# Transformer block on one core: V computed once per token and spread by SBUF to SBUF transfers, probabilities packed at 48 keys a block

## The reference, cut to what matters

```python
q, k, v = split_heads(xn @ qkv_w + qkv_b)            # 16 heads, head_dim 16
k_pad = jnp.pad(k, ((0, 0), (7, 7), (0, 0)))
v_pad = jnp.pad(v, ((0, 0), (7, 7), (0, 0)))
idx = jnp.arange(L)[:, None] + jnp.arange(15)[None, :]
scores = einsum('bld,blwd->blw', q, k_pad[:, idx]) / 4
out = einsum('blw,blwd->bld', softmax(scores, -1), v_pad[:, idx])
return merge_heads(out) @ proj_w + proj_b
```

## Time and profile before

| | |
|---|---|
| median of three runs | 2178.18 us |
| the profiled execution | 2176.03 us |
| its span, first to last instruction | 2174.3 us |
| around the span | 1.7 us |
| PE busy, PE weight loads busy | 95%, 87% |
| DVE, ACT, POOL busy | 73%, 50%, 48% |
| granted TensorE clock, mean | 0.99 |
| distance from one step to the next in the steady part | 131.3 us |

### The profile page before, as it was taken

How to read it: one execution, slowest core, us unless ns; L and a number is a source line. 1 busy time by engine, 2 the same in 40 slices (tenths; PEclk the granted TensorE clock), 3 DMA queues, 4 the chain that set the end, 5 groups by cost and what they waited for, 6 DMA issues and landing times.

```text
span 2174.3 us, 39417 instructions
## 1 busy us (share of the span) xinstructions
PE 2068.2 (95%) x13985; PEld 1883.4 (87%) x13985; DVE 1585.7 (73%) x3535; ACT 1095.1 (50%) x1716; POOL 1054.2 (48%) x993
## 2 busy tenths in 40 slices
PE   5689999999999999999999999999999999999999
PEld 4578898888988888898888989888898898988888
DVE  7568686786868768686785868868687786867843
ACT  3245554545555545554545545545455555545444
POOL 7544355544454534455444555534455443555435
PEclk9699999999999999999999999999999999999999
DMA  2111111111101111011111111111011111111111
GB/s 87 39 35 40 44 36 35 50 40 44 39 26 49 50 44 35 30 47 43 49 40 40 40 30 49 40 54 30 25 54 45 45 40 45 35 35 50 40 49 49
DMA packets 128881, 92.14 MB, mean 42 GB/s; under 512 B 9673, under 2 KB 127662, under 8 KB 128686
## 3 DMA queue, kind: packets, MB, share of 16 engines
q1 hardware_dynamic: 128686, 89.62, 13.9%
HBM read 81.20 MB, written 8.39 MB: 41 GB/s over the span
## 4 chain that ended last, share of the span: by engine, by line
PE 66%; DVE 24%; issue 6%; POOL 3%; ACT 1%; DMA 0%; DVEq 0%; ACTq 0%; POOLq 0%
PE psB L234 33%; PE psA L234 24%; DVE tm L606 10%; PE psA L1021 4%; DVE hr_lo L511 4%; PE psA L942 3%; DVE tm L622 1%; PE psA L1048 1%; DVE acc L525 1%; DVE smax L582 1%; DVE vb L562 1%; DVE smax L589 1%; DVE y L614 1%; DVE z_lo L539 1%; DVE st L501 1%
## 5 line engine op out<-in xcount | busy, mean ns | idle before, releaser
L511 DVE TENSOR_TENSOR hr_lo<-hf,hr_hi 128x512 fp32r<-128x512 f32 x512 | 469.3, 917 | 433.3 <-ACT hr_hi L828 431.2
L828 ACT ACTIVATE hr_hi<-hf 128x512 fp32r<-128x512 f32 x512 | 323.4, 632 | 316.4 <-PE psB L234 223.3
L403 POOL TENSOR_SCALAR wx_hi<-raw 128x512 fp32r<-128x512 f32 x256 | 168.5, 658 | 481.3 <-PE psB L234 470.4
L405 POOL TENSOR_TENSOR wx_lo<-raw,wx_hi 128x512 fp32r<-128x512 f32 x256 | 384.3, 1501 | 21.4
L824 ACT ACTIVATE hf<-psB,b1x 128x512 f32<-128x512 f32 x256 | 175.7, 686 | 278.5 <-PE psB L234 264.4
L418 POOL TENSOR_SCALAR kb<-kT,gmask 128x384 f32<-128x384 f32 x128 | 159.0, 1257 | 287.9 <-ACT kT L844 287.9
L234 PE MATMUL psB<-wx_hi,hr_hi 128*128 128x256 f32 x1024 | 288.8, 282 | 0.2
L234 PE MATMUL psB<-wx_hi,hr_lo 128*128 128x256 f32 x1024 | 287.1, 280 | 0.0
L234 PE MATMUL psB<-wx_lo,hr_hi 128*128 128x256 f32 x1024 | 287.0, 280 | 0.0
L606 DVE TENSOR_TENSOR tm<-psA,rinv 32x64 f32<-32x64 f32 x1024 | 225.8, 220 | 25.2 <-PE psA L1048 11.4
L234 PE MATMUL psB<-z_hi,wx_hi 128*128 128x512 f32 x512 | 212.3, 415 | 0.0
(11 more groups left out here) (158 smaller groups left out, 5470.7 us busy)
## 6 DMA issues: line engine op xcount, KB each, us to landing
raw<-in_L_ffn_W1e SPq DMA_DIRECT2D x256, 128.0 KB, 2.2
raw<-in_L_ffn_W2e SPq DMA_DIRECT2D x256, 128.0 KB, 2.1
xin<-in_L_attn_x SPq DMA_DIRECT2D x16, 512.0 KB, 3.7
out_x<-acc SPq DMA_DIRECT2D x32, 256.0 KB, 2.7
raw<-in_L_attn_fc_w SPq DMA_DIRECT2D x8, 256.0 KB, 2.8
raw<-in_L_ffn_W1m SPq DMA_DIRECT2D x4, 256.0 KB, 2.7
raw<-in_L_ffn_W2m SPq DMA_DIRECT2D x4, 256.0 KB, 2.8
raw<-in_L_attn_qkv_w SPq DMA_DIRECT2D x4, 192.0 KB, 4.5
```

What stands on the lines that cost most here:

```text
L403: g.tensor_scalar(wx[0][:, s, :], raw[:, s, :], 1.0, 0.0, ALU.mult, ALU.add).then_inc(w_hi.sem, 1)
L405: g.tensor_tensor(wx[1][:, s, :], raw[:, s, :], wx[0][:, s, :].bitcast(f32), ALU.subtract).then_inc(w_lo.sem, 1)
L511: v.tensor_tensor(hr[1][:, c % 2, :], hf[:, c % 3, :], hr[0][:, c % 2, :].bitcast(f32), ALU.subtract).then_inc(h_lo.sem, 1)
L828: a.activation(hr[0][:, c % 2, :], hf[:, c % 3, :], ACT.Copy).then_inc(h_hi.sem, 1)
```

## The change

V is computed once per token: two calls of `values`, n = 0 and 1 at q 3 and 4, each for two adjacent tiles of 128 tokens. DVE adds the bias in one instruction of 128x512 a call and writes `vs`, tokens on partitions. Then SP issues six transfers from `vs` to `vb` (`windows`), at its q 3, behind the loads of that q; all six increment one semaphore, and PE's `attend(t, 0)` waits for all of them. They have 7, 41, 48, 48, 39 and 9 partitions, with 12 or 16 runs of 64 floats (256 B) on each. A block has 48 places in `pr`, so two blocks are 96 columns: `turn` makes 96 rows, ACT copies 96, and `attend` works on 96 partitions of `pT` and `vb`. The blocks of a unit stand in their natural order (`place` is gone). The mask `keep` and the zero fill of `pr` are gone.

```diff
-        vb = sb("vb", [P, NB // 2, KD * G, P])
-        pr = sb("pr", [P, 2, 2, G, 4, 64])
+        vs = sb("vs", [P, NT, D])
+        vb = sb("vb", [PK, 2, NT, KD * G, P])
+        pr = sb("pr", [P, 2, 2, G, 4, KW])
...
+            def windows(t):
+
+
+                sp.wait_ge(vs_s.sem, vs_s.all(t))
+                if t:
+                    sp.wait_ge(av.sem, av.all(t - 1))
+                for half, j, key, at, n, tiles, back in (
+                        (0, 0, 0, P - RAD, RAD, range(1, NT), 1), (0, 0, RAD, 0, KW - RAD, range(NT), 0),
+                        (0, 1, 0, QB - RAD, KW, range(NT), 0), (1, 0, 0, 2 * QB - RAD, KW, range(NT), 0),
+                        (1, 1, 0, 3 * QB - RAD, QB + RAD, range(NT), 0), (1, 1, QB + RAD, 0, KW - QB - RAD, range(0, NT - 1), -1)):
+                    sp.dma_start(vb[KW * j + key:KW * j + key + n, half, tiles[0]:tiles[-1] + 1, :, 64 * j:64 * j + 64].rearrange("p i g n -> p (i g) n"),
+                                 vs[at:at + n, tiles[0] - back:tiles[-1] + 1 - back, :].rearrange("p i (g n) -> p (i g) n", n=64)
+                                 ).then_inc(vb_in.sem, 16)
...
+                    if q == 3 and t < ROWS:
+                        if t == 0:
+                            sp.wait_ge(zeroed.sem, 1)
+                        windows(t)
...
-            g.memset(pr[:, :, :, :, :, :], 0.0).then_inc(zeroed.sem, 1)
-            g.memset(vb[:, :, :, :], 0.0).then_inc(zeroed.sem, 1)
+            g.memset(vb[:, :, :, :, :], 0.0).then_inc(zeroed.sem, 1)
...
             def values(t, n):
                 v.wait_ge(val.sem, val.at(t, n))
                 if t:
...
+                    v.wait_ge(vb_in.sem, vb_in.all(t - 1))
+                v.tensor_tensor(vs[:, 2 * n:2 * n + 2, :], psA[:, 2, :].rearrange("p (i n) -> p i n", n=D),
+                                bv[:, :].unsqueeze(1).to_broadcast([P, 2, D]), ALU.add).then_inc(vs_s.sem, 1)
...
-                    base = LEFT - RAD + (4 * n + j) * QB
+                    to = LEFT + (2 * n + j) * P
...
                 for g in range(G):
                     pe.wait_ge(pT_s.sem, pT_s.at(t, 2 * u + g))
                     if g == 0:
-                        pe.wait_ge(vb_s.sem, vb_s.at(t, (11, 15, 15, 15)[u]))
+                        pe.wait_ge(vb_in.sem, vb_in.all(t))
...
                     elif q == 7:
                         turn(t, 0)
-                        pe.wait_ge(vb_s.sem, vb_s.at(t, 7))
-                        values(t, 2)
...
                     elif q == 10:
                         scores(t, 3)
-                        pe.wait_ge(att.sem, att.at(t, 0))
-                        values(t, 3)
```

More of the change, by code:

```diff
@@ L36, in build @@
     KW = 48
+    PK = 2 * KW
     G = 2
@@ L110, in build @@
         ones = one[:, :].to_broadcast([1, P])
-        keep = sb("keep", [P, 3])
         bv = sb("bv", [P, D])
@@ L241, in chunk_weights @@
             return ([[w[:, s, k * P:(k + 1) * P] for w in wx] for k in range(KD)], [w[:, s, KD * P:] for w in wx])
-        def place(j):
-            return 2 * (j % 2) + j // 2
         def unit_scores(u):
-            return pr[:, u % 2, :, :, :, 0:KW].rearrange("p t g b k -> p (t g b) k")
+            return pr[:, u % 2, :, :, :, :].rearrange("p t g b k -> p (t g b) k")
         HALVES = (range(0, NT // 2), range(NT // 2, NT))
@@ L600, in attend @@
                         src = psA[QB * h:QB * h + QB, 2:4, :].rearrange(
-                            "p g (t j s n) -> p g t j s n", t=2, j=2, s=2)[:, :, :, b % 2, b // 2, HD * h:HD * h + HD]
+                            "p g (t j s n) -> p g t j s n", t=2, j=2, s=2)[:, :, :, b // 2, b % 2, HD * h:HD * h + HD]
                         dst = tm[QB * b:QB * b + QB, 2 * th:2 * th + 2, c * P:(c + 1) * P].rearrange(
                             "p t (g n) -> p g t n", g=G)[:, :, :, HD * h:HD * h + HD]
-                        w = rinv[QB * h:QB * h + QB, u, :, :, :].rearrange("p t g b -> p g t b")[:, :, :, place(b)]\
+                        w = rinv[QB * h:QB * h + QB, u, :, :, :].rearrange("p t g b -> p g t b")[:, :, :, b]\
                             .unsqueeze(3).to_broadcast([QB, G, 2, HD])
@@ L869, in turned @@
                         a.wait_ge(av.sem, av.at(t - 1, 6 + g))
-                    a.activation(pT[:, g, :, :].rearrange("p j q -> p (j q)"), psA[:, g, :], ACT.Copy).then_inc(pT_s.sem, 1)
+                    a.activation(pT[0:PK, g, :, :].rearrange("p j q -> p (j q)"), psA[0:PK, g, :], ACT.Copy).then_inc(pT_s.sem, 1)
             for t in range(ROWS + 1):
@@ L996, in values @@
                 for j in range(2):
-                    base = LEFT - RAD + (4 * n + j) * QB
+                    to = LEFT + (2 * n + j) * P
                     for k in range(KD):
-                        last = three(pe, psA[:, 2, j * D:(j + 1) * D], [z[:, k, base:base + P] for z in zT], [w[:, k, 2 * D:] for w in wqkv],
+                        last = three(pe, psA[:, 2, j * D:(j + 1) * D], [z[:, k, to:to + P] for z in zT], [w[:, k, 2 * D:] for w in wqkv],
                                      k == 0, k == KD - 1)
@@ L1019, in scores @@
                         b = 4 * h + j
-                        dst = psA[:, h, 0:4 * G * KW].rearrange("p (g b k) -> p g b k", g=G, k=KW)[:, :, place(j), :]
+                        dst = psA[:, h, 0:4 * G * KW].rearrange("p (g b k) -> p g b k", g=G, k=KW)[:, :, j, :]
                         last = pe.matmul(dst, qm[:, th, b, :], kb[:, th, b, :].rearrange("p (g k) -> p g k", g=G), start=True, stop=True)
@@ L1032, in turn @@
                     for j in range(NP_):
-                        last = pe.transpose(psA[:, g, j * P:(j + 1) * P], pr[:, th, j // 2, g, 2 * (j % 2):2 * (j % 2) + 2, :].rearrange("p b k -> p (b k)"), ident[:, :])
+                        last = pe.transpose(psA[0:PK, g, j * P:(j + 1) * P], pr[:, th, j // 2, g, 2 * (j % 2):2 * (j % 2) + 2, :].rearrange("p b k -> p (b k)"), ident[:, :])
                     last.then_inc(trp.sem, 1)
@@ L1047, in attend @@
                     for j in range(NP_):
-                        last = pe.matmul(psA[:, 2 + g, j * P:(j + 1) * P], pT[:, g, j, :], vb[:, th * NP_ + j, c * G + g, :], start=True, stop=True)
+                        last = pe.matmul(psA[:, 2 + g, j * P:(j + 1) * P], pT[0:PK, g, j, :], vb[:, j % 2, 2 * th + j // 2, c * G + g, :], start=True, stop=True)
                     last.then_inc(av.sem, 1)
```

16 lines of the change are left out of this document (4 added, 12 removed).

## The result

The changed kernel takes 2325.1 us (median of four runs, 2323.2 to 2326.2) against 2178.1 us, 1.0675 times the time of before, 95% interval 1.0657 to 1.0694: slower by 147 us. The forecast was 2325.

What follows compares the result with a forecast made beforehand. PE's own work was taken to set a steady row, so new waits are paid in full. The profiled 2176.0 us plus 43.9 for row 0 plus 105 for 15 steady rows gave 2325 us; range 2275 to 2445.

Steps and rivals of the forecast that it cites:

- One engine for 41 partitions: The six transfers: engines get equal numbers of partitions, so 41, a prime, goes to one engine with 656 packets.
- Rival A: The six transfers: all engines share them evenly, 188 packets each; 2162 us, faster by 0.6%; chance 0.10.
- rule of 260 packets on the fullest engine: Transfers in steady rows: below about 260 packets on the fullest engine no steady row stalls.
- The start: SP's q 3: transfers stand behind load 7, issued every 0.57 us; PE comes to `attend(0)` at 435.26, 1.51 us earlier.
- The price of a packet: The transfers: 19 ns per 256 B packet, 812 packets on the fullest engine 15.4 us, plus 1.75 us fixed.
- Rival B: The transfers: a 256 B packet costs as much as one of 512 B, 28 ns; 2442 us; chance 0.17.
- The idles behind the stall: PE in the weighted sums of a steady row: DVE's head start removes two idles, minus 2.2 us.
- The clock: PE behind the stall: granted clock 0.50 for 3.5 us of work, adding 1.65 us to a steady row.
- A steady row: Counted on PE: 9.0 later, minus `values(3)` 1.5, minus idles 2.2, plus clock 1.65; +7.0 us, +105 in 15 rows.
- The other count, on DVE: Steady row: DVE starts 8.5 us later, minus 2.0 for the placements; sum 6.5 us.
- Row 0: Transfers wait in SP's queue behind the last dense piece and land at 88.9; transposes start at 117.1, 43.9 us later.
- No effect: Transposes and sum over keys, denser `mask`, `shift` and `exp`, and expert loads behind the transfers: 0.

Runs made afterwards that it cites:

- 40 + 1: Changed kernel with the transfer of 41 partitions cut into 40 and 1: 2179.7 us, 1.0009 of before.
- the doubled transfer: Changed kernel with the first transfer of 48 partitions cut into 47, also a prime, and 1: 2487.9 us.
- the kernel with the cut widths: Changed kernel with the transfers of 41 and 39 partitions cut into 32 + 9 and 32 + 7: 2187.4 us, 1.0049 of before.
- the last experiment: Kernel with split, early transfers and row 0 mended, plus DVE's gathers of units 2 and 3 ahead of that q's rounding difference: 2112.6 us, 0.9702 of before.
- the filler: Changed kernel with 28 useless matmuls of 512 columns on PE ahead of the first weighted sum of rows 1 to 15: 2284.2 us.
- early transfers: Changed kernel with the six transfers issued ahead of load 7 in steps from 1 on: 2169.9 us, 0.996 of before.
- either repair: Changed kernel with either the 41 and 39 partitions cut in two (2187.4 us) or the transfers issued ahead of load 7 (2169.9 us).
- both together with row 0's: Changed kernel with split transfers, issued ahead of load 7, and row 0's behind the first eight dense pieces: 2124.9 us, 0.9756 of before.

## Why the prediction was right, and where its terms were not

**The bound.** Right: PE's own work sets a steady row, so removed matmuls pay in full and a new wait costs in full. Without transfers, and with row 0's 40 us in it, the kernel takes 2169.3 us; 2178.1 + 40.1 - 45 is 2173. The 4 us between them stay open.

**One engine for 41 partitions.** Right, and the step that decided. It was an inference from a count of completion packets; the flat 18 GB/s, the 62 completion packets a row, the cuts into 32 + 9 and 40 + 1 and the doubled transfer bear it out. Rival A, even sharing, is the kernel with the cut widths, whose transfers are nearly even: 2187 us, not the 2162 I gave it. The sign of that rival was wrong too: with the late place it is no faster than before. Its own rule of 260 packets on the fullest engine failed too: the cut transfers have 216 there, and every row still stalls, because eight issues of 0.89 us make the last one late.

**The start.** Right: the transfers follow load 7, and PE arrived within 0.3 us of the time I gave, counted from `turn(0)` (8.42 us in row 3 for 8.17).

**The price of a packet.** Mis-sized. I took 19 ns, a duration from a straight line between 11 and 28 ns; the duration is 18, the long transfer's packets follow each other every 14.5 ns, and where all engines work it is 21. Against it, an issue of such a transfer takes about 0.9 us instead of 0.57, and SP stood, which I hadn't seen coming. Together the landing came 15.4 us after the first issue where I had 17.7, and the stall is 7.66 us on average, 8.80 in row 3, where load 7 itself went out slowly, for 10.5 forecast. This term was 2.8 us too large. Rival B, 28 ns, is out.

**The idles behind the stall.** Wrong, the step as I put it: "minus the two idles 2.2, which DVE's head start removes". They are there to a hundredth, 1.12 and 1.02 us for 1.15 and 1.03. A head start at the first unit doesn't reach them: each idle arises between two neighbours, PE's sum and DVE's gather, and the last experiment removes most of one by changing DVE's order. 2.2 us too little.

**The clock.** The mechanism was right, the size wrong: 1.65 us forecast, 2.7 measured by the filler. I had read the low clock's length from row 0 as 3.5 us of work; here it covers the 5.4 us of work up to 502.8. Row 0 before had shown as much: the transposes at 89.71, ahead of the stretch that I read, ran at 0.50 too, 1.97 us of work that I left out.

```profile
89.00:92.00 3.00, 1.97 (x8) 1.57 (x8) 0.93 (x2) 1.04 (x2) 2.92 (x4) 0.50 0.46 161
```

I had also priced the first sum at 2.85 us, a row during which the clock changed; at the low clock throughout it takes 3.75.

**A steady row.** 7.66 - 3.0 + 2.7 = 7.4, against 7.3 measured; forecast 10.5 - 3.0 - 2.2 + 1.65 = 7.0. The stall was 2.8 us too large, the idles (2.2) and the clock (1.05) together 3.25 too small, so by luck only 0.3 to 0.4 is left. The starts in row 3 give the same: from the first sum to the transposes it is 33.62 us for 32.48 before, 1.14 more, which is the 1.51 of `values(3)` less and 2.65 of clock more. The other count, on DVE, gave 6.5. It took the 2.0 us of placements off as if DVE set the pace up to the transposes; from its first gather to them it is 29.83 us (501.15 to 530.98) for 29.10 before (440.15 to 469.25), not 2.0 less.

**Row 0.** 40.1 us late, 43.9 forecast. SP came to the transfers 2.4 us earlier (68.77 for 71.19), they landed 2.2 us sooner behind that (15.5 us for 17.7), and the chain of the four units took 29.0 us for 28.2. The first was wrong in its reason: "Nothing of that waits for PE, so it stays", and of the constants removed on POOL, "before a wait for ACT: 0". In row 0 that wait itself hangs on POOL, for DVE waits for POOL's last constant before it can make the input of the projections. First before, then changed:

```profile
16.25 0.81 DVE L533 TENSOR_SCALAR pT<-psA,smallT 128x512 f32<-128x512 f32 x1 [4.47 <-POOL iota L380]
```

```profile
15.22 0.81 DVE L545 TENSOR_SCALAR pT<-psA,smallT 128x512 f32<-128x512 f32 x1 [3.80 <-POOL iota L393]
```

That is 1.03 us earlier, some 0.7 for the three constants; the input also arrived 0.35 us earlier. POOL's splits, which set SP's pace in row 0, begin 1.75 us earlier (35.13 for 36.88) and end 2.55 us earlier. I put the rest down to DVE's fewer placements and to shorter instructions on POOL; no experiment tests that.

**No effect.** The 96 partitions of transposes and sums, the denser `pr` and the loads behind the transfers: right, no cost shows, by the kernels with early transfers and without any in steady rows.

## What to carry to other kernels

A transfer's partition count decides how many engines carry it. Before moving work from a busy engine to transfers, see that each count has a large divisor up to 16, cut those that haven't, count 0.9 us for each issue, and look at what stands behind a long one in the issuing queue. Then ask where in that queue the transfers stand, since they inherit every wait ahead of them: here either repair alone won back the 147 us or nearly so, and both together with row 0's turned 6.8% slower into 2.4% faster. A stall of 7 us costs more than its length, for the clock falls in it (2.7 us here); and a total that is right doesn't show that its terms are, so check each against its row.

## What the runs showed of the hardware

- The issuing queue stands at the transfer behind a long one: 8.37 us of the 13.08 for six issues, 8.39 and 10.53 us of 23.20 with a second long one; with the long one last, six issues take 5.38. Every transfer that stood needs the busy engine too, so no run tells whether one that doesn't would pass.
- On one engine that works alone, 256 B packets from SBUF to SBUF follow each other every 14.5 ns (18 GB/s), though each is recorded as 18 ns; with all sixteen at work each engine takes 21 ns for one (762 packets in 1 us).
- The issue of a transfer with 84 to 768 short runs takes about 0.9 us of SP's time on average (eight in 7.09 us), that of a weight load 0.37 us, one every 0.57 us.
- In row 3, where PE had stood for 8.80 us, the granted clock was 0.50 (1.2 GHz of 2.4) for the 5.4 us of work up to 502.8; after an idle of 1.84 us in the kernel with the cut widths the sums took what they take at 1.00, and after one of 1.73 us in the kernel with 40 and 1 they took 3.32 us and the clock was 0.50 in part. So the length of an idle alone doesn't tell here whether the clock falls. 6.7 us of useless matmuls in the wait made the kernel 41 us faster.
